# Self-attention of a decoder layer: projections that hold the weights, and rotation halves swapped by VectorE's shuffle

## The reference, cut to what matters

```
Q = (x @ Wq.T).reshape(B, T, 16, 32).transpose(0, 2, 1, 3)
K = (x @ Wk.T).reshape(B, T, 4, 32).transpose(0, 2, 1, 3)
V = (x @ Wv.T).reshape(B, T, 4, 32).transpose(0, 2, 1, 3)
Q, K = apply_rope(Q), apply_rope(K)   # [x1*cos - x2*sin, x2*cos + x1*sin], halves of 16
scores = einsum('bkgtd,bksd->bkgts', Q.reshape(B, 4, 4, T, 32), K) / sqrt(32)
attn = softmax(where(causal, scores, min))
out = einsum('bkgts,bksd->bkgtd', attn, V) ... @ Wp.T
```

## Time and profile before

| | |
|---|---|
| median of 3 runs | 561.2 us (558.74 to 561.34) |
| span of the profiled execution | 562.4 us |
| PE busy | 527.4 us, 94% |
| DVE, ACT, POOL busy | 400.9, 304.3, 283.0 us |
| granted TensorE clock | full in every slice of the span |
| self-attention stage | about 0 to 165 us |

### The profile page before, as it was taken

The page is one execution under the profiler, slowest core; times in us unless marked ns, Lnnn a source line. Parts: engine busy times, 40 slices in busy tenths (PEclk is TensorE's granted clock), DMA queues, the critical chain, the costliest instruction groups (busy, mean ns, idle before and its releaser), DMA issues. The chain is left out here.

```text
span 562.4 us, 9748 instructions
## 1 busy us (share of the span) xinstructions
PE 527.4 (94%) x3451; PEld 371.3 (66%) x3451; DVE 400.9 (71%) x909; ACT 304.3 (54%) x701; POOL 283.0 (50%) x360
## 2 busy tenths in 40 slices
PE   5889999999989999999999999999999999989875
PEld 4657776766767666677666776668677776865432
DVE  6575897896676798766876567884676657787663
ACT  3164745646655777656676366774567644422330
POOL 0569643465706666903666035772155533772550
PEclk9999999999999999999999999999999999999999
DMA  8976644776350720432892323243210047127528
GB/s 250 273 268 211 223 140 149 271 206 197 154 194 29 219 81 2 75 106 65 230 247 66 99 69 87 39 75 76 75 43 4 1 150 299 61 79 162 140 86 261
DMA packets 46242, 76.77 MB, mean 137 GB/s; under 512 B 20082, under 2 KB 30100, under 8 KB 45300
## 3 DMA queue, kind: packets, MB, share of 16 engines
q1 hardware_dynamic: 42948, 63.60, 36.3%
q0 software_dynamic: 2224, 10.73, 8.4%
q10 hardware_dynamic: 1024, 1.84, 1.0%
HBM read 57.36 MB, written 28.23 MB: 152 GB/s over the span
## 5 line engine op out<-in xcount | busy, mean ns | idle before, releaser
L2148 POOL TENSOR_TENSOR xprob<-xprob,erec 128x375 f32<-128x375 f32 x112 | 94.0, 844 | 129.1 <-DVE erec L1766 128.7
L1350 ACT ACTIVATE xprob<-s_ps,nmax 128x375 f32<-128x375 f32 x112 | 64.1, 573 | 55.3 <-DVE nmax L1761 53.5
L1761 DVE TENSOR_REDUCE nmax<-s_ps 128x1 f32<-128x375 f32 x112 | 59.4, 537 | 0.0
L2141 POOL TENSOR_TENSOR prob<-prob,rec 112x1792 f32<-112x1792 f32 x8 | 25.5, 3186 | 50.4 <-DVE rec L1669 50.2
L62 PE MATMUL s_ps<-kvt,qt_hl 128*128 128x376 f32 x112 | 48.1, 429 | 2.0 <-ACT xprob L1350 1.3
L1744 DVE SCALAR_TENSOR_TENSOR pt_hl<-f_ps,pt_hl 125x384 f16<-125x384 f32 (+1 forms) x62 | 38.0, 613 | 13.8 <-ACT pt_hl L1328 12.6
L62 PE MATMUL k_ps<-ow,ctx_hl 128*128 128x512 f16 (+1 forms) x104 | 39.6, 381 | 0.0
L64 PE MATMUL k_ps<-ow,ctx_hl 128*128 128x512 f16 (+1 forms) x104 | 39.4, 379 | 0.0
L63 PE MATMUL k_ps<-ow,ctx_hl 128*128 128x512 f16 (+1 forms) x104 | 39.4, 379 | 0.0
L63 PE MATMUL s_ps<-kvt,qt_hl 128*128 128x376 f32 x112 | 37.4, 334 | 0.0
L64 PE MATMUL s_ps<-kvt,qt_hl 128*128 128x376 f32 x112 | 37.4, 334 | 0.0
(11 more groups left out here) (383 smaller groups left out, 1494.8 us busy)
## 6 DMA issues: line engine op xcount, KB each, us to landing
w<-w_dram SPq DMA_DIRECT2D x6, 1024.0 KB, 9.8
raw_b<-in_raw SPq DMA_DIRECT2D x8, 640.0 KB, 5.6
raw_m<-in_raw SPq DMA_DIRECT2D x8, 576.0 KB, 4.9
raw_q<-in_raw SPq DMA_DIRECT2D x8, 512.0 KB, 7.1
ow_dram<-bw_sb SPq DMA_DIRECT2D x8, 512.0 KB, 5.8
ow_raw<-ow_dram SPq DMA_DIRECT2D x8, 512.0 KB, 3.3
qw_raw<-aw_dram SPq DMA_DIRECT2D x16, 256.0 KB, 3.1
w_dram<-in_w POOLq DMA_DIRECT2D x8, 512.0 KB, 5.7
```

What stands on the lines that cost most here:

```text
L1350: act.activation(xprob[z][:, 0:L], s_bank(n, k)[:, 0:L], ACT.Exp, bias=nmax[:, z:z + 1], accum_out=esum[:, z:z + 1]).then_inc(xexp_done, 1)
L1761: dve.tensor_reduce(nmax[:, z:z + 1], s_bank(n, k)[:, 0:L], X, ALU.max, negate=True).then_inc(xmax_done, 1)
L2141: pool.tensor_tensor(prob[q][:, :, :, :], prob[q][:, :, :, :], rec[q][:, :, :].unsqueeze(3).broadcast_to([T, PER, GROUPS, T]), ALU.mult).t ...
L2148: pool.tensor_tensor(xprob[z][:, 0:L], xprob[z][:, 0:L], erec[:, z:z + 1].broadcast_to([128, L]), ALU.mult).then_inc(xp_ready, 1)
```

## The change

A table of cosines and one of sines are loaded with each row repeated four times (128 features), turned once by PE (`turn_tables`), and copied by ACT, so that features lie on the partitions. The projection now holds 128 columns of the weights in the array and streams the tokens of both batches of a round (224 columns): queries take four such tiles, keys one and values one. Queries come out of it with features on the partitions, and so are never turned; only the values are turned (`turn_v`, two transposes a round). Query heads are laid so that a tile holds one head of each of the four key groups. `project_q(i+1)` stands where `project_qkv(i+1, 0)` stood, `project_kv(i)` where `project_qkv(i, 1)` stood. The rotation takes three parts `z` a round: tiles 0 and 1, tiles 2 and 3, and the keys. For each, DVE multiplies by the cosines and swaps the halves of 16 partitions by a stream shuffle from PSUM, and POOL multiplies by the sines and adds. `rope(i+1, 0)` and `rope(i+1, 1)` stand where `rope(i+1, 0)` stood, `rope(i, 2)` where `rope(i, 1)` stood. `turn_qk` and `copy_qk` are gone, and `scores(i, q)` waits for all three parts of the round. Key heads are no longer repeated.

```diff
-            sp.dma_start(qcos[:, :], a["qcos"]).then_inc(tab_loaded, 16)
-            sp.dma_start(qsin[:, :], a["qsin"]).then_inc(tab_loaded, 16)
+            for n, name in enumerate(("qcos", "qsin")):
+                sp.dma_start(tables[:, n], a[name].unsqueeze(1).broadcast_to([T, 128 // HD, HD])).then_inc(tables_ready, 16)
...
-            def project_qkv(i, q):
...
+            def project_part(tiles, bank, k, first):
+
+                for j, m in enumerate(tiles):
+                    out = bank[:, j * 2 * T:(j + 1) * 2 * T]
+                    for n, (w, x) in enumerate(((0, 0), (0, 1), (1, 0))):
+                        mm = pe.matmul(out, wqkv_hl[:, w, k, m * 128:(m + 1) * 128], xt_hl[:, x, k, :],
+                                       start=(first and j == 0 and n == 0), stop=(k == KC - 1 and n == 2), skip_group_check=True)
+                return mm
+
+            def project_q(i):
+                pe.wait_ge(xt_low, 2 * i + 2)
...
+                for z in range(2):
+                    for k in range(KC):
+                        mm = project_part((2 * z, 2 * z + 1), f_ps[z], k, k == 0)
+                    mm.then_inc(qk_done, 1)
+
+            def project_kv(i):
+
+                if i == 0:
+                    pe.wait_ge(wqkv_low, KC + 1)
+                for z, done in ((0, qk_done), (1, vt_done)):
+                    pe.wait_ge(rope_read, 3 * i + z + 1)
+                    for k in range(KC):
+                        mm = project_part((PER + z,), f_ps[z], k, k == 0)
+                    mm.then_inc(done, 1)
+
+            def turn_v(i):
+                pe.wait_ge(vt_copied, i + 1)
+                for q in range(2):
+                    mm = pe.transpose(f_ps[1][0:T, 2 * T + q * 128:2 * T + (q + 1) * 128], vt_sb[:, q * T:(q + 1) * T], ident[:, :])
+                mm.then_inc(v_turned, 1)
...
             def scores(i, q):
...
-                pe.wait_ge(qkt_copied, 2 * b + 2)
...
+                pe.wait_ge(roped, 3 * i + 3)
+                tok = slice(q * T, (q + 1) * T)
...
+            def rope(i, z):
+
+                made, rest, n = roped_parts(i, z)
+                dve.wait_ge(qk_done, 3 * i + z + 1)
+                wait(dve, s_done, 2 * (i - 1))
+                wait(dve, roped, 3 * (i - 1) + z + 1)
+                src = f_ps[z % 2][:, 0:n * T].rearrange("p (n t) -> p n t", n=n)
+                dve.tensor_tensor(made, src, qcos[:, :].unsqueeze(1).broadcast_to([128, n, T]), ALU.mult)
+                dve.stream_shuffle(rest, src, ROTATED).then_inc(rope_read, 1)
...
+            def rope_add(i, z):
+
+                made, rest, n = roped_parts(i, z)
+                pool.wait_ge(rope_read, 3 * i + z + 1)
...
+                own.link(pool.tensor_tensor(rest, rest, qsin[:, :].unsqueeze(1).broadcast_to([128, n, T]), ALU.mult))
+                pool.tensor_tensor(made, made, rest, ALU.add).then_inc(roped, 1)
...
                 if more:
                     rope(i + 1, 0)
+                    rope(i + 1, 1)
```

More of the change, by code:

```diff
@@ L377, in attention @@
         wp_hl, x2n = sb("wp_hl", [128, 2, KC, C], F32R, room), pairs("x2n", [T, C], F32, room)
-        v_sb = [sb(f"v_sb{z}", [T, GROUPS, HD], F32, room) for z in range(4)]
+        v_sb = sb("v_sb", [T, 4, GROUPS * HD], F32, room)
         prob, probt = pairs("prob", [T, PER, GROUPS, T], F32, room), sb("probt", [T, PER, GROUPS, T], F32, room)
@@ L459, in attention, with by_head, by_place, roped_parts @@
     wo = raw_b[:, R_KV:R_KV + R_WO].rearrange("p (i n) -> p i n", i=2)
+    ROTATED = [(d + HH) % HD for d in range(HD)]
     def is_last(i):
         return i == ROUNDS
+    def by_head(w):
+        return w.rearrange("p (g j d) -> p g j d", g=GROUPS, j=PER)
+    def by_place(w):
+        return w.rearrange("p (j g d) -> p g j d", g=GROUPS, j=PER)
+    def roped_parts(i, z):
+        if z < 2:
+            return qt[i % 2][:, 2 * z:2 * z + 2, :].rearrange("p j (q t) -> p (j q) t", q=2), \
+                turned[:, 2 * z:2 * z + 2, :].rearrange("p j (q t) -> p (j q) t", q=2), 4
+        return kt[i % 2][:, :].rearrange("p (q t) -> p q t", q=2), turned[:, PER, :].rearrange("p (q t) -> p q t", q=2), 2
     def cols(bank, rows=128):
@@ L741, in turn, with turn_tables @@
                 mm.then_inc(done, 1)
+            def turn_tables():
+                pe.wait_ge(tables_ready, 32)
+                for n in range(2):
+                    mm = pe.transpose(b_ps[0][:, n * T:(n + 1) * T], tables[:, n].rearrange("t r d -> t (r d)"), ident[0:T, 0:T])
+                mm.then_inc(tables_ready, 1)
             def scores_weight(p):
@@ L785, in turn_x @@
                 pe.wait_ge(xn_ready, 2 * i + q + 1)
[L786 removed]
+                if i and q == 0:
+                    pe.wait_ge(rope_read, 3 * i)
+                if i and q == 1:
+                    pe.wait_ge(v_copied, i)
                 turn(f_ps[q], xn[q], xt_done)
[L789 to L804 removed]
@@ new lines, in project_q @@
+            def project_q(i):
+                pe.wait_ge(xt_low, 2 * i + 2)
+                if i == 0:
+                    for k in range(KC):
+                        pe.wait_ge(wqkv_low, k + 1)
+                        for z in range(2):
+                            mm = project_part((2 * z, 2 * z + 1), f_ps[z], k, k == 0)
+                            if k == KC - 1:
+                                mm.then_inc(qk_done, 1)
+                    return
+                for z in range(2):
+                    for k in range(KC):
+                        mm = project_part((2 * z, 2 * z + 1), f_ps[z], k, k == 0)
+                    mm.then_inc(qk_done, 1)
@@ L828, in scores @@
                               start=True, stop=False, skip_group_check=True)
-                pe.wait_ge(qkt_copied, 2 * b + 2)
-                for g in range(GROUPS):
-                    for j in range(PER):
-                        mm = pe.matmul(s_ps[0:T, j, g * T:(g + 1) * T],
-                                       qt[j * HD:(j + 1) * HD, g, :], kt[j * HD:(j + 1) * HD, g, :],
-                                       start=False, stop=(g == GROUPS - 1), skip_group_check=True)
+                pe.wait_ge(roped, 3 * i + 3)
+                tok = slice(q * T, (q + 1) * T)
+                for j in range(PER):
+                    for g in range(GROUPS):
+                        mm = pe.matmul(s_ps[0:T, g, j * T:(j + 1) * T],
+                                       qt[i % 2][g * HD:(g + 1) * HD, j, tok], kt[i % 2][g * HD:(g + 1) * HD, tok],
+                                       start=False, stop=(j == PER - 1), skip_group_check=True)
                 mm.then_inc(s_done, 1)
@@ L861, in apply_probs @@
                         mm = pe.matmul(b_ps[q][j * HD:(j + 1) * HD, g * T:(g + 1) * T],
[L862 removed]
+                                       v_sb[:, c % 4, g * HD:(g + 1) * HD], probt[:, g, j, :], start=True, stop=True,
                                        skip_group_check=True)
@@ L1139, in _ @@
             keep_warm(16)
-            project_qkv(0, 0)
+            project_q(0)
+            turn_tables()
             for i in range(ROUNDS):
@@ L1145, in _ @@
                     scores_weight(p)
-                project_qkv(i, 1)
+                project_kv(i)
                 if i:
@@ L1181, in _ @@
                 if more:
-                    project_qkv(i + 1, 0)
+                    project_q(i + 1)
                 else:
@@ L1543, in _ @@
                 copy_out_weight(p + 1, 1)
-                if more:
-                    copy_v(i + 1, 0)
-                else:
+                if not more:
                     pair_high(0, 0)
```

131 lines of the change are left out of this document (44 added, 87 removed).

## The result

The changed kernel takes 566.25 us (median of 8 runs, 562.91 to 568.45), the kernel before 560.27 us (8 runs, 558.74 to 562.97): a ratio of 1.0098, 95% interval 1.0076 to 1.0121. It is 6.0 us slower. I had forecast 562.8 us, no measurable change, in a range up to 566.0; the outcome is above both. Where a text says that one changed kernel is faster than another, medians are compared, whose intervals are some ±1 to 2 us.

A forecast was written before the change was run, and what follows sets the result against it. PE looks full, but DVE is level in first halves and the limit in second ones. Terms +1.3 + 0.1 + 1.0 − 0.95 + 0.9 − 0.9 = +1.45, say +1.6: 562.8 us, range 557.5 to 566.

The forecast's parts named there:

- (c): Round 0, second half: DVE has no residual work yet, PE sets the pace, project_q(1) is longer: +1.0 us.
- the only stage that the change touches: Self-attention stage, 0 to 165 us, four rounds of two batches; all terms of the forecast lie in it.
- (a): Round 0, tables: 896 packets for 224 in a full queue delay raw_b and ctx_raw: +1.3 us, all on the path.
- (b): Round 0: scores(0,0) needs all three parts from POOL, 5.8 us, before DVE takes the scores up: +0.1 us.
- PE's projections: Each round: 0.109 us a matmul, project_q 5.3 us and project_kv 2.7, where one batch's projection took 4.3.
- First halves: Up to scores(i,0), rounds 1 to 3: PE waits about 1.5 us for DVE's shift; −0.2, −0.2, −0.55, sum −0.95 us.
- Second halves: From scores(i,0) to scores(i,1), rounds 1 and 2: DVE's longer rotation delays kvt_hl: +0.45 us each, +0.9.
- Round 3's second half: With turns gone ahead of apply_probs, the queue up to the exponential that DVE waits for moves up: −0.9 us.
- Rival A: PE is the bound: rounds 1 to 3 give 2.1 us each, −6.3, so 554.9 us; chance 0.17.
- Rival B: Slower: a shuffle costs 1.15 us or more, four lie ahead of kvt_hl, +2.2, 565.0 us; chance 0.16.
- C: Round 0: the tables' packets cost 2.5 us or more and delay raw_b, 564 to 566 us; chance 0.10.

The follow-up runs named there:

- all moves: Changed kernel with probabilities turned in the stand, kvt_hl between rotations, round 1 tokens early, 14 idle matmuls, 7 fillers, wp_hl work earlier: 559.40 us, ratio 0.9962.
- the new order in before: Kernel before with two of four turns of the probabilities ahead of scores_weight in the first halves: 567.43 us, ratio 1.0112.

## Why the prediction was wrong

**The failed step** is (c) of round 0, "PE sets the pace, and `project_q(1)` is 1.0 longer": +1.0, and from `scores_weight` on it measured +2.80. With the stands filled it is +1.15, so the work was sized right; the missing 1.65 us is the granted clock, at 0.50 for some 3 us. I counted PE's stands as time that passes, and no more, and put the clock behind them at nothing. The change takes the turns of queries and keys away from PE behind `scores(0,0)`, so the stand at `scores_weight` grew from 1.49 to 2.56 us. The profile of before had a sign of it in plain sight: five matmuls there whose result nobody reads, kept at that one place. Taking them out costs before 1.65 us in that half. The loss varies: with the change and five fillers, r0h2 is 18.96, 21.17, 18.69 and 20.02 us in four profiles, 19.7 on the mean, against 17.27 with the clock at 1.00.

**A second step failed with it,** and its cause is open. I took the stage up to 165 us as "the only stage that the change touches", and put the rest at nothing. The part behind the last cast of `o_sb` is longer with the change in all nine profiles that have no idle matmuls in the first halves: 16.7 us on the mean, against 14.8 in the four of before, so +1.9. SP's issue of the four `got` transfers takes 1.74 us in before and 2.3 to 2.8 in seven of the nine; why is not known.

**Sum.** With the stands filled it is +1.7 us in the time and +2.16 at the end of the stage, against +1.6 and +1.45 forecast. The result lies 6.0 us over its own before, 4.4 more than the forecast. My estimate from the means above is that 2.4 of these are the clock in round 0 and 1.9 the last part; the first is shown, the second only located. (Against the figure of 562.8 the miss is 3.45, as the median of before fell by 0.9 with more runs.)

**Round 0, (a) and (b): right at the cut that they were for,** 1.42 us against 1.4. The end of `scores(0,0)` moved more, by 2.08, and there POOL and not `raw_b` set it: PE waits 0.99 us for POOL's `kt`. POOL started its rotation 0.97 us later than before (27.40), since its context came later, and needed 6.02 us for it, where I had 5.8. In before DVE took the scores up 0.85 us behind their end, now 0.19, which hides the rest.

**PE's projections: right, a little low.** I took 0.109 us a matmul. The 48 of `project_q` that start at 43.16 end before the next row at 49.00, at most 0.122 each; 5.55 us in the run with early tokens is 0.116. The Trainium skill (TensorE: Matmul & The Clock Gate, "LDWEIGHTS (loading the stationary operand)") prices a load of 128 columns at about 107 ns. The steps measured here lie 8 to 14% above that.

**First halves: the wait right, the gain not.** The wait of 1.43 us is there three times, released by DVE's `prob`. Gains are 0 in rounds 1 and 2, where I had −0.2 from `aw_sb`. But `aw_sb` did not hold that end: it now starts 9.28 us behind the start of `scores_weight` (67.05 and 57.77 us) and before 10.50, and `scores(1,0)` starts 11.58 us behind it in both. PE's own queue of steps from `scores_weight` on sets that length: the turns of queries and keys (0.77 us) are gone from it, the turn of the values (0.36) and a wait for ACT's `at_sb` (0.22) came in, and its waits for ACT's copies of the turned probabilities stayed. Round 3 gave 0.3 of the 0.55.

**Second halves: right in place and sign,** +0.34 of +0.45. The run with `kvt_hl` moved gives just these 0.35 us back, and the run with two shuffles shows DVE as the pace. A product and a shuffle out of PSUM are 0.55 and 0.56 us a step. The Trainium skill (VectorE: DVE Perf Modes, "The perf-mode tier table") has 2400 ns for a shuffle of 2048 elements and 2293 for an fp32 product. In the prediction I used this gap of 0.1 us at 448 columns without scaling it; by elements it is an estimate of 0.02 us. Here the durations differ by 0.06 (0.67 and 0.61) and the steps by 0.01.

**Round 3's second half: right,** −0.92 of −0.9.

**Rival A** (PE as the bound, −6.3) fell as expected, by the wait that it had against it. There was something in it: once the stands are put to use, the stage ends at 157.5 us, against 162.3 before. Rival B (a dear shuffle) and C (packets of 2.5 us or more) gave a time near the measured one, but a shuffle costs 0.56 us, and `raw_b` came 1.2 us later.

## What to carry to other kernels

When a change takes work from TensorE ahead of a wait, ask not only whether the wait swallows the gain but what the engine's clock does behind a longer stand: list the stands of TensorE before and after, and look for filler work that someone has placed. A saving that a wait swallows is still there; move independent work into the stand, and judge an order only together with the durations it was made for. And compare the end of the kernel too, where nothing was edited, over several profiles: part of a loss can lie there.

## What the runs showed of the hardware

- **A stand costs more than its length, and not always.** The granted clock fell to 0.50 behind PE's stands of 2.56 us (the changed kernel), 2.38 and 3.62 (512 B tables), 3.64 (early tokens), 2.10 (packets added to before), 2.44 (before without fillers), 2.21 and 3.62 (`kvt_hl` moved), 2.15 (all moves), and behind 1.20 and 1.40 with little work between (11 fillers) or 1.68 (two turns moved). It stayed at 1.00 behind 1.85 us in the changed kernel and 1.76 with the tables laid out, behind one stand of 1.91 us, and fell behind another of 1.91. In two profiles it also fell for some 7 us from about 482 and 486 us, where PE had stood for no more than 0.30 us since 476, so a stand is not its only occasion. Where it fell it stayed low for some 3 us (the changed kernel) to 7 us (512 B tables), and matmuls took up to twice as long.
- **Time goes with clock from run to run.** Over 214 runs of fifteen kernels, with a level for each kernel, a microsecond of lost clock, (1 − mean clock) times the span, goes with 0.61 us of time; the rest scatters by 1.1 us. That is no proof of cause; for round 0 the idle matmuls are.
- **Open: the last 17 us.** The clock also falls in the last 10 us of many profiles, in a part that the change doesn't touch. In the changed kernel's profile it is 0.66 from 555 to 560 us behind a wait of 2.51 us for `got`; the longest such wait in the profile of before is 0.74. With the stands of the first stage filled, 10 of 12 runs had a mean clock of 0.995 or more. Why these transfers come later with the change was not tried.
- **The same DVE instruction has several lengths.** The two `xn` products take 1.63 us at 65.04 in the changed kernel, beside POOL's parts of 224 columns, 2.83 in before at 60.87, and 3.88 us at 60.99 with the new order in before, both beside POOL's additions of 512 columns, the last beside its `normalise` too. No run separates the two engines, so that POOL is the reason is an inference.
- **Small packets.** With 672 more packets of 128 B in a full queue, what stood behind them came 1.0 to 1.6 us later, in one profile; my estimate from the earlier trace rows was 1.3, or 1.9 ns each.
